# Last stage of a two-layer gated transformer: scale the second expert product after it leaves PSUM, and sum residual and gated row on ScalarE

## The reference

```
x = x + tanh(g_ffn[1]) * ffn(layernorm(x))

ffn(xf):
    scores, idx = top_k(xf @ gate_W + gate_b, 2)
    weights = softmax(scores)
    expert e: h = relu(layernorm(xf @ W1[e] + b1[e]) * g1[e] + be1[e])
              y = layernorm(h @ W2[e] + b2[e]) * g2[e] + be2[e]
    out = sum over the two chosen experts of weight * y
    return out + xf
```

## Time and profile before

| | |
|---|---|
| median of 3 runs | 2147.1 us (2144.46 to 2152.93) |
| profiled execution | 2151.43 us, span 2149.6 us |
| granted clock, mean over the span | 0.984 |
| busy: PE, PEld, DVE, ACT, POOL | 2058.6 (96%), 1795.7 (84%), 1737.7 (81%), 1394.5 (65%), 1269.6 (59%) us |
| chain that ended last | PE 65%, DVE 15%, POOL 9%, issue 6%, DMA 3%, ACT 1% |

### The profile page before, as it was taken

How to read it: one execution, slowest core, us unless ns; L and a number is a source line. 1 busy time by engine, 2 the same in 40 slices (tenths; PEclk the granted TensorE clock), 3 DMA queues, 4 the chain that set the end, 5 groups by cost and what they waited for, 6 DMA issues and landing times.

```text
span 2149.6 us, 57692 instructions
## 1 busy us (share of the span) xinstructions
PE 2058.6 (96%) x19788; PEld 1795.7 (84%) x19788; DVE 1737.7 (81%) x4788; ACT 1394.5 (65%) x2978; POOL 1269.6 (59%) x2056
## 2 busy tenths in 40 slices
PE   6999999999699999999699999999899999999997
PEld 5888888888599999999588888888788888888885
DVE  5889888888588888888577787777588888888886
ACT  4766666666487877878366666666566666666663
POOL 5787888887300000000477878777378878878786
PEclk9999999999799999999899999999999999999998
DMA  7555221221466666666322222222100000000000
GB/s 230 187 180 166 67 65 61 69 64 53 158 239 226 247 223 246 221 244 213 133 69 71 71 75 71 75 71 66 45 23 30 29 28 29 30 30 30 30 26 18
DMA packets 151664, 226.11 MB, mean 105 GB/s; under 512 B 20454, under 2 KB 135786, under 8 KB 141036
## 3 DMA queue, kind: packets, MB, share of 16 engines
q1 hardware_dynamic: 145260, 205.99, 28.5%
q0 software_dynamic: 6144, 16.79, 2.5%
HBM read 153.77 MB, written 68.94 MB: 104 GB/s over the span
## 4 chain that ended last, share of the span: by engine, by line
PE 65%; DVE 15%; POOL 9%; issue 6%; DMA 3%; ACT 1%; POOLq 0%; SPq 0%; DVEq 0%; ACTq 0%
PE ps L1255 10%; PE ps L1271 10%; PE ps L1127 10%; PE ps L1112 6%; DVE u2g L1328 4%; PE ps L1066 4%; PE ps L1203 3%; PE ps L1215 3%; DVE h_st L1297 3%; PE ps L1159 3%; POOL k_rs L614 2%; PE ps L1083 2%; PE ps L1060 2%; PE ps L1096 2%; PE ps L1026 2%
## 5 line engine op out<-in xcount | busy, mean ns | idle before, releaser
L1397 DVE TENSOR_REDUCE nmax<-ps 128x16 f32<-128x2048 f32 x128 | 292.4, 2284 | 29.4 <-PE ps L1083 29.0
L874 ACT ACTIVATE prob_t<-ps 128x2048 f32<-128x2048 f32 x128 | 240.9, 1882 | 77.8 <-PE ps L1066 77.8
L696 POOL COPY slot_in<-slot_all 128x1 int32<-128x1 int32 x64 | 11.4, 179 | 472.9 <-DMA eo_d<-eo 472.9
L1026 PE MATMUL ps<-w2f,a_t 128*128 128x256 f32 x1024 | 233.3, 381 | 0.0
L1255 PE MATMUL ps<-xgt_hi,w_hl 128*128 128x256 f32 x1248 | 230.0, 282 | 1.0 <-DVE xgt_lo L1662 1.0
L1271 PE MATMUL ps<-w_hl,hid_hi 128*128 128x256 f32 x1248 | 226.9, 284 | 0.0
L1026 PEld LDWEIGHTS ps<-w2f,a_t 128*128 128x128 f32 x1024 | 190.9, 191 | 23.8
L670 POOL TENSOR_TENSOR km_r<-qk,cst 128x512 fp32r<-128x512 f32 x128 | 133.7, 1044 | 127.7 <-ACT qk L864 127.7
L946 ACT ACTIVATE hid<-ps,b_in 128x256 f32<-128x256 f32 x312 | 146.0, 469 | 82.6 <-PE ps L1255 67.2
L1255 PEld LDWEIGHTS ps<-xgt_hi,w_hl 128*128 128x128 f32 x1248 | 195.5, 189 | 1.4 <-issue 1.4
L1271 PEld LDWEIGHTS ps<-w_hl,hid_hi 128*128 128x128 f32 x1248 | 191.5, 188 | 0.0
(11 more groups left out here) (229 smaller groups left out, 6247.7 us busy)
## 6 DMA issues: line engine op xcount, KB each, us to landing
w_raw<-in_w_dram SPq DMA_DIRECT2D x78, 1024.0 KB, 6.8
c_t<-in_ctx_in_dram SPq DMA_DIRECT2D x128, 128.0 KB
x_d<-x SPq DMA_DIRECT2D x128, 128.0 KB
slots_d<-zeros SPq DMA_DIRECT2D x12, 1024.0 KB, 6.2
eo_d<-zeros SPq DMA_DIRECT2D x12, 1024.0 KB, 5.3
xg<-slots_d SPq DMA_DIRECT2D x39, 256.0 KB, 2.7
eo_d<-eo SPq DMA_DIRECT2D x39, 256.0 KB, 2.2
x_in<-in_x_dram SPq DMA_DIRECT2D x64, 128.0 KB
```

Of the source, the lines that this page charges most:

```text
L874: nc.scalar.activation(prob_t[:].rearrange("p a k -> p (a k)"), scores.rearrange("p a k -> p (a k)"), ACT.Exp, scale=SOFT).then_inc(y["exp ...
L1026: mm = pe.matmul(dst, a_t[:, b.parity, e, c, :], w2f[:, e, c, :], start=False, stop=True, skip_group_check=True)
L1397: nc.vector.tensor_reduce(nmax[:, b.parity, :, 0:4], scores.rearrange("p a (r k) -> p a r k", k=P), AX_X, ALU.max, negate=True).then_inc(y ...
```

## The change

The scale `k_rw` is no longer applied when the second product is read from PSUM. VectorE multiplies the product with `g2_in` alone, in two instructions of two experts each (`out_of_psum`), one behind each half of `k_st`, so one batch earlier than before; `u2g` gets a second buffer. ScalarE then scales the four parts in place in SBUF with `k_rw`, after `xft_hi` and before `z1`.

The residual and the gated normalised row become one sum. VectorE makes a scale and a shift, `y_sb` (one plus gate times `frs` scale, gate times `frs` shift), in two 128x1 instructions between `gate_mix` and `h_st`; they wait for `frs` of batch s + 1. ScalarE makes `xg_sum` from `x3` with them, between `xf` and `xft_hi`. `mixed` is then a plain sum of PSUM and `xg_sum`. GpSimd's sum with `x3` is gone, `u2s` moves behind `h_rs`, and GpSimd's `frs` waits for both `xf` and `xg_sum` of the batch before. The aggregation `k_mv` waits for the first `k_rs` of the batch before.

```diff
@@ -312,14 +312,14 @@
         k_mv = psb("k_mv", [P, E1, 2])
         k_rs = psb("k_rs", [P, 2, E1])
         k_rw = psb("k_rw", [P, E1])
-        u2g = psb("u2g", [P, E1, D])
+        u2g = psb("u2g", [P, 2, E1, D])
         u2s = psb("u2s", [P, 2, D])
-        u2t = psb("u2t", [P, D])
         rest = psb("rest", [P, 2, D])
         mixed = psb("mixed", [P, 2, D])
         x4 = psb("x4", [P, 2, D])
-
-        late = 4096 + 4 * E1 * 6 // 4 + E1 * 2 + 2 * E1 + E1 + 4 * D + 2 * D + D + 2 * D + 2 * D + 2 * D
+        xg_sum = psb("xg_sum", [P, 8, D])
+
+        late = 6912 + 4 * E1 * 6 // 4 + E1 * 2 + 2 * E1 + E1 + 4 * D + 2 * D + D + 2 * D + 2 * D + 2 * D
         psb("gap1", [P, ATTENTION_WORDS - late])
         w1f = psb("w1f", [P, C, E1, D])
         w1_hi = psb("w1_hi", [P, C, E1, D], F32R)
@@ -347,6 +347,7 @@
         fmv = psb("fmv", [P, 2])
         frs = psb("frs", [P, 4])
         xf = psb("xf", [P, 8, D + 1])
+        y_sb = psb("y_sb", [P, 2])
         xft_hi = psb("xft_hi", [P, 2, C, P], F32R)
         xft_lo = psb("xft_lo", [P, 2, C, P], F32R)
         gpart = psb("gpart", [P, E1])
@@ -416,10 +417,10 @@
 
         f = signals(
             "f_", {},
-            dict(st=2, rstd=4, xf_done=1, x_turned=1, x_hi_done=1, x_lo_done=1, gates_done=1, gates_half=1, gates_read=1, gate_steps=4,
+            dict(st=2, rstd=4, xf_done=2, x_turned=1, x_hi_done=1, x_lo_done=1, gates_done=1, gates_half=1, gates_read=1, gate_steps=4,
                  gexp_done=1, gate_mix=5, gwt_done=1, gw_turned=1, gw_t_done=1, up1_done=2, h_stats=8, h_rstd=2, z_act=4,
-                 z_turned=2, a_done=8, down1_done=2, k_stats=8, k_rstd=3, u_done=4, be_done=1, mixed_done=1, halved=1,
-                 summed=2, mix=1))
+                 z_turned=2, a_done=8, down1_done=2, k_stats=8, k_rstd=3, u_done=2, u_scaled=4, be_done=1, mixed_done=1, halved=1,
+                 summed=1, y_scaled=2, mix=1))
         f.update({name: arrival("f_" + name, ring=ring) for name, ring in dict(x3_came=8, x4_stored=2).items()})
         s_fw = sem("s_fw")
         s_first_hi = sem("s_first_hi")
@@ -608,7 +609,7 @@
                     st = f["k_rstd"]
                     pool.wait_ge(f["k_stats"].of(b), f["k_stats"].at(b))
                     if (b - 1).begun:
-                        pool.wait_ge(f["u_done"].of(b - 1), f["u_done"].at(b - 1))
+                        pool.wait_ge(f["u_scaled"].of(b - 1), f["u_scaled"].at(b - 1))
                     nc.gpsimd.tensor_tensor(k_rs[:, 0, :], k_mv[:, :, 1], eps.to_broadcast([P, E1]), ALU.add).then_inc(st.sem, 1)
                     pool.wait_ge(st.of(b), st.at(b, 1))
                     nc.gpsimd.tensor_tensor(k_rs[:, 1, :], k_rs[:, 0, :], neg_half.to_broadcast([P, E1]), ALU.pow).then_inc(st.sem, 1)
@@ -634,12 +635,6 @@
                     if (b - 2).begun:
                         pool.wait_ge(f["gw_turned"].of(b - 2), f["gw_turned"].at(b - 2))
                     nc.gpsimd.tensor_tensor(gw8[:, b.parity, 0:E1], gwa[:], gwb[:], ALU.add).then_inc(f["gwt_done"].sem, 1)
-                b = s - 2
-                if b.within(B):
-                    pool.wait_ge(f["u_done"].of(b), f["u_done"].at(b))
-                    if (b - 1).begun:
-                        pool.wait_ge(f["summed"].of(b - 1), f["summed"].at(b - 1))
-                    nc.gpsimd.tensor_tensor(u2s[:], u2g[:, 0:2, :], u2g[:, 2:4, :], ALU.add).then_inc(f["halved"].sem, 1)
                 b = s
                 if b.within(B):
                     st = f["h_rstd"]
@@ -651,10 +646,14 @@
                     nc.gpsimd.tensor_tensor(h_rs[:, 1, :], h_rs[:, 0, :], neg_half.to_broadcast([P, E1]), ALU.pow).then_inc(st.sem, 1)
                 b = s - 2
                 if b.within(B):
+                    pool.wait_ge(f["u_scaled"].of(b), f["u_scaled"].at(b))
+                    if (b - 1).begun:
+                        pool.wait_ge(f["summed"].of(b - 1), f["summed"].at(b - 1))
+                    nc.gpsimd.tensor_tensor(u2s[:], u2g[:, b.parity, 0:2, :], u2g[:, b.parity, 2:4, :], ALU.add).then_inc(f["halved"].sem, 1)
+                b = s - 2
+                if b.within(B):
                     pool.wait_ge(f["halved"].of(b), f["halved"].at(b))
-                    nc.gpsimd.tensor_tensor(u2t[:], u2s[:, 0, :], u2s[:, 1, :], ALU.add).then_inc(f["summed"].sem, 1)
-                    pool.wait_ge(f["summed"].of(b), f["summed"].at(b, 1))
-                    nc.gpsimd.tensor_tensor(rest[:, b.parity, :], u2t[:], x3[:, b.off % 8, :], ALU.add).then_inc(f["summed"].sem, 1)
+                    nc.gpsimd.tensor_tensor(rest[:, b.parity, :], u2s[:, 0, :], u2s[:, 1, :], ALU.add).then_inc(f["summed"].sem, 1)
                 b = s - 3
                 if b.within(B):
                     pool.wait_ge(f["summed"].of(b), f["summed"].at(b))
@@ -772,11 +771,21 @@
                         act.wait_ge(f["mixed_done"].of(b - 8), f["mixed_done"].at(b - 8))
                     nc.scalar.activation(xf[:, b.off % 8, 0:D], x3[:, b.off % 8, :], ACT.Identity, scale=frs[:, 1:2], bias=frs[:, 3:4])\
                         .then_inc(f["xf_done"].sem, 1)
+                    act.wait_ge(f["y_scaled"].of(b), f["y_scaled"].at(b))
+                    nc.scalar.activation(xg_sum[:, b.off % 8, :], x3[:, b.off % 8, :], ACT.Identity, scale=y_sb[:, 0:1], bias=y_sb[:, 1:2])\
+                        .then_inc(f["xf_done"].sem, 1)
                     act.wait_ge(f["x_turned"].of(b), f["x_turned"].at(b))
                     if (b - 2).begun:
                         act.wait_ge(f["gates_done"].of(b - 2), f["gates_done"].at(b - 2))
                     nc.scalar.activation(xft_hi[:, b.parity].rearrange("p c k -> p (c k)"), ps[:, 0, 0:D], ACT.Copy)\
                         .then_inc(f["x_hi_done"].sem, 1)
+                b = s - 2
+                if b.within(B):
+                    act.wait_ge(f["u_done"].of(b), f["u_done"].at(b))
+                    act.wait_ge(f["k_rstd"].of(b), f["k_rstd"].at(b))
+                    for e in range(E1):
+                        nc.scalar.activation(u2g[:, b.parity, e, :], u2g[:, b.parity, e, :], ACT.Copy, scale=k_rw[:, e:e + 1])\
+                            .then_inc(f["u_scaled"].sem, 1)
                 b = s
                 if b.within(B):
                     act.wait_ge(f["h_rstd"].of(b), f["h_rstd"].at(b))
@@ -1005,12 +1014,12 @@
                         pe.wait_ge(y1["x1_done"].of(At(0, B - 1)), y1["x1_done"].at(At(0, B - 1)))
                     for e in (0, 2):
                         if (b - 1).begun:
-                            pe.wait_ge(f["u_done"].of(b - 1), f["u_done"].at(b - 1, e + 2))
+                            pe.wait_ge(f["u_done"].of(b - 1), f["u_done"].at(b - 1, e // 2 + 1))
                         pe.matmul(ps[:, 6 + e // 2, :], ones2[:], b2_hl[:, e:e + 2, :].rearrange("p e n -> p (e n)"),
                                   start=True, stop=False, skip_group_check=True)
                 b = s + 1
                 if b.within(B):
-                    pe.wait_ge(f["xf_done"].of(b), f["xf_done"].at(b))
+                    pe.wait_ge(f["xf_done"].of(b), f["xf_done"].at(b, 1))
                     if (b - 1).begun:
                         pe.wait_ge(f["x_lo_done"].of(b - 1), f["x_lo_done"].at(b - 1))
                     for c in range(C):
@@ -1303,6 +1312,14 @@
                 for e in range(E1):
                     nc.vector.bn_aggr(mv[:, e, :], st[:, e, :]).then_inc(sig.sem, 1)
 
+            def out_of_psum(b, half):
+
+                if (b - 2).begun:
+                    dve.wait_ge(f["halved"].of(b - 2), f["halved"].at(b - 2))
+                two = slice(2 * half, 2 * half + 2)
+                nc.vector.tensor_tensor(u2g[:, b.parity, two, :].rearrange("p e n -> p (e n)"), ps[:, 6 + half, :],
+                                        g2_in[:, two, :].rearrange("p e n -> p (e n)"), ALU.mult).then_inc(f["u_done"].sem, 1)
+
             def fstep(s):
                 b = s - 1
                 if b.within(B):
@@ -1319,15 +1336,13 @@
                     nc.vector.tensor_scalar(gwa[:], iota_e[:, 0:E1], gidx[:, 0:1], gw[:, 0:1], ALU.is_equal, ALU.mult).then_inc(gm.sem, 1)
                     dve.wait_ge(gm.of(b), gm.at(b, 3))
                     nc.vector.tensor_scalar(gwb[:], iota_e[:, 0:E1], gidx[:, 1:2], gw[:, 1:2], ALU.is_equal, ALU.mult).then_inc(gm.sem, 1)
-                b = s - 2
-                if b.within(B):
-                    dve.wait_ge(f["k_rstd"].of(b), f["k_rstd"].at(b))
+                b = s + 1
+                if b.within(B):
+                    dve.wait_ge(f["rstd"].of(b), f["rstd"].at(b))
                     if (b - 1).begun:
-                        dve.wait_ge(f["halved"].of(b - 1), f["halved"].at(b - 1))
-                    for e in range(E1):
-                        nc.vector.scalar_tensor_tensor(out=u2g[:, e, :], in0=ps[:, 6 + e // 2, (e % 2) * D:(e % 2 + 1) * D],
-                                                       scalar=k_rw[:, e:e + 1], in1=g2_in[:, e, :],
```

(11 more changed lines are left out.)

## The result

The changed kernel takes **2201.8 us** (median of 4 runs, 2201.14 to 2204.39) against 2146.6 us for the kernel before (4 runs, 2144.46 to 2152.93): ratio **1.0259**, 95% interval 1.0246 to 1.0272, so slower by 2.6%. The profiled execution took 2201.14 us, its span is 2199.3 us and its mean granted clock 0.986, against 2151.43, 2149.6 and 0.984.

A forecast was written before the change was run, and what follows sets the result against it. VectorE's loop with GpSimd (9.01 us a step) was the bound, TensorE's floor of 8.81 close by. Steps of 10.09 against 9.07, +1.02 times 61, start +1.5, end -1.5, gave +62 on 2147.1: 2209 us, range 2188 to 2240.

The forecast's parts named there:

- The mechanism: VectorE, last stage: the new `frs` wait uses up what the removed `u2g` and its wait gave; `h_st` stays at 3.65 us.
- K: Zero of the step's timeline in the last stage: the start of `k_mv` on VectorE; K+3.65 means 3.65 us later.
- The products: VectorE's two 128x512 products before `k_mv`: 0.61 us each from start to start, bounds 0.40 and 0.69, adding 0.61 and 0.51.
- The end: Last steps of the stage: VectorE has no `frs` to wait for and one sum fewer precedes the last `x4`: -1.5 us.
- The start's +1.5: First steps of the stage: products without a wait to give back add some 1.5 us.
- What was costed at nothing: `xg_sum` and scalings on ScalarE, sums on GpSimd: hidden, scalings by 0.5 us before `z`, GpSimd by 0.7 before `k_rs`.
- Faster: Rival: VectorE's wait goes and TensorE bounds the last stage; 15 us off, 2132 us, chance 4%.
- Its formula: VectorE's step is t + 0.03 + 0.26 + 6.42 us, t being when `frs` is done after `k_mv` starts; 3.36 in the trace.
- No change: Rival: `frs` done near 2.4 us after `k_mv`, or the wait half gone and products hidden; 2147 us, chance 3%.
- ScalarE late: Rival: ScalarE's scalings end late and GpSimd's sums push the next `k_rs`; 24 us more, 2233 us, chance 9%.
- The clock falls: Rival: TensorE's clock drops in its new gaps, the second product takes 5.3 us; +107 us, 2254 us, chance 5%.
- one ring: The loop from `k_mv` through GpSimd's `k_rs`, `k_rw`, `frs` to `y_sb` and VectorE's queue to the next `k_mv`: 10.07 us.

The follow-up runs named there:

- the product half with one sum more: Kernel before with only the unscaled product and ScalarE's scalings (no `y_sb`, no `xg_sum`), plus one idle 256-column sum on GpSimd: 2221.4 us, ratio 1.0350.
- the product half alone: Kernel before with only the unscaled product on VectorE and the four scalings on ScalarE; no `y_sb`, no `xg_sum`, GpSimd's sum kept: 2184.7 us, ratio 1.0174.
- the product half with `frs` first: Kernel before with only the unscaled product and ScalarE's scalings, and GpSimd's `frs` placed ahead of `k_rs` and `k_rw`: 2127.8 us, ratio 0.9900.

## Why the prediction was right

**The mechanism** of the changed kernel came as told. The new wait took exactly what the removed `u2g` and its wait gave: `h_st` at K+3.62, where it was at K+3.65. The terms, by the timeline above:

| term | predicted | measured |
|---|---|---|
| `k_mv` to `y_sb` | 0.46 + 2.93 = 3.39 | 3.37 |
| two `y_sb` | 0.26 | 0.25 |
| `h_st` to the next `k_mv` | 5.36 - 0.06 + 0.61 + 0.51 = 6.42 | 6.37 |
| the step, mean of 61 | 10.09 | 10.02 |
| 61 steps against before | +62 | +58 |
| the end | -1.5 | -5.1 |

**The products.** Taken 0.61 from start to start, they measured 0.59 (1958.46 to 1959.05, and 1960.25 to 1960.84); the row of the same shape in another stage was the right one to read, and 0.69 and 0.40, the bounds, were both far off.

**The end** was the worst term. Before, TensorE stood 2.20 us for `u2g`, and then did its last long product in 5.30 us, at a granted clock of 0.57 from 2130 to 2134 us:

```profile
2128.13 0.49 PE L1009 MATMUL ps<-b_hl,ones 128*128 128x512 f32 x1 [2.20 <-DVE u2g L1328]
```

In the changed kernel the wait for `u2g` is gone, and the same product takes 3.72, at a granted clock of 1.00 (2180 to 2184 us):

```profile
2180.50 3.72 PE L1035 MATMUL ps<-w2f,a_t 128*128 128x256 f32 x16 [0.26 <-ACT a_t L815]
```

The prediction counted one wait and one sum, and not what the scaled read of PSUM held up in the last steps. The start's +1.5 can't be told from the 3 us between two executions.

**What was costed at nothing** stayed hidden. `xg_sum` fits between `xf` and `xft_hi`. The scalings run 0.40 apart, as taken (four take 1.69 us), from K+4.93 to K+6.6; `z` waits 0.30 behind them, so they are hidden by 0.3 and not 0.5. GpSimd has 0.82 to spare, predicted 0.7, and two sums more on it confirm that (step +0.24 for 1.14 us of work). TensorE stands 0.86 before the turning of `xf` in the step shown and 0.77 on average, predicted 0.9.

**The rivals.** *Faster* did not occur because `frs` is done at t = 3.34, as before. Its formula did: with `frs` first, `y_sb` starts 1.41 after `k_mv`, VectorE's ring is 1.41 + 0.25 + 6.37 = 8.03, shorter than TensorE's floor, and the step is 8.74; 2124 us where the rival said 2132. The 8.81 read as that floor was somewhat too high: it was the shortest step of a kernel in which TensorE was not always the last, and with `frs` first the distances between first matmuls are 8.74 to 8.77 from the third step on. *No change* and *ScalarE late* did not occur. *The clock falls*: it did not, though TensorE stands in every step; the granted clock is 1.00 from 1600 to 2100 us. It is so too in the product half with one sum more, where that gap is 1.25 us a step. The Trainium skill (TensorE: Matmul & The Clock Gate, "A second HAM failure mode: psum-queue depth-cycling") tells of a bf16 kernel in which frequent short idles of TensorE make the gate swing; at 0.77 us in 10.0, and at 1.25 in 10.3, no such swing shows here. That the loss comes from the order of GpSimd's queue was the forecast itself, and one exchange of blocks turns it.

**What the prediction lacked** shows only in the experiments. It spoke of one ring and of covers, each with a size. But a cover of 0.82 us in a step of 9.99 is a ring of about 9.2, the second ring beside it is one of about 9.1 (9.7 in the product half alone, which has a sum more), and others lay near 9.6 as soon as `y_sb` or the scalings moved. So the wait before `y_sb` is what sets the step of the changed kernel, but taking it away is worth less than the 55 us: with `y_sb` later 24 us come back, and the product half alone, which has no `y_sb`, still loses 38. Three expectations (`y_sb` later, the product half alone, the scalings first) missed by 9 to 29 us for this reason: each removed one ring and took the path through `xf`, the second product and `k_st`, at 9.2 to 9.5 us, for the next. The exchange on GpSimd shortens the path to `frs`, and `xf` behind it, for every ring at once.

**Open.** Whether `y_sb` behind the gates' sum would reach TensorE's floor with `xg_sum` at another place, such as behind the scalings, wasn't tried. TensorE's work is the same in the product half with `frs` first, and it is busy all the time there too, but the step is 8.79 and not 8.74; why is not known.

## What to carry to other kernels

When an edit makes an engine wait for a new result, look at what stands ahead of that result in its producer's queue, not only at its own cost: here 1.5 us of `k_rs` and `k_rw`, waiting for `k_mv`, made `frs` late, and exchanging the two blocks turned +2.6% into -1.1%. The order that is right follows the waits: in the kernel before, the same exchange cost 2.3%. After removing a wait, convert every hidden stretch into the length of its own ring (step less idle time), because the longest of those is the next step length. One idle instruction added to the engine in question tells within one run whether that engine has room; by which way the ring goes, only the chain and the waits of that run tell.

## What was not expected of the hardware

GpSimd's sum of 128x256 took 0.57 us from start to start (0.61 busy) where both operands were the same 256 columns (`be2_in`), and 0.68 (0.73 busy) for `rest` and `x4` with two different ones; no run shows whether that is the reason. TensorE's granted clock stayed at 1.00, its 2.4 GHz level, with 0.77 us of idle time before the turning of `xf` in a mean step of 10.0, and with 1.25 in one of 10.3.
